# Two attention layers: the maxima over keys turned by VectorE's 32x32 transposes in place of TensorE's 128x128 transposes

## The reference

```python
q = conv1x1(xn, wq, bq).reshape(B, N, C)
k = conv1x1(xn, wk, bk).reshape(B, N, C)
v = conv1x1(xn, wv, bv).reshape(B, N, C)
scores = jnp.einsum('bnc,bmc->bnm', q, k) * scale
attn = jax.nn.softmax(scores, axis=-1)
out = jnp.einsum('bnm,bmc->bnc', attn, v).reshape(B, H, W, C)
return conv1x1(out, wp, bp) + x
```

## Time and profile before

| | |
|---|---|
| median of 3 runs | 264.88 us (264.76 to 265.24) |
| the profiled execution | 265.16 us |
| its span, first to last instruction | 263.3 us |
| granted clock of TensorE | 1.00 |
| busy: TensorE, VectorE, ScalarE, GpSimd | 257.6, 178.2, 151.3, 110.5 us |

### The profile page before, as it was taken

The page is one execution under the profiler, slowest core; times in us unless marked ns, Lnnn a source line. Parts: engine busy times, 40 slices in busy tenths (PEclk is TensorE's granted clock), DMA queues, the critical chain, the costliest instruction groups (busy, mean ns, idle before and its releaser), DMA issues.

```text
span 263.3 us, 4614 instructions
## 1 busy us (share of the span) xinstructions
PE 257.6 (98%) x1662; PEld 233.8 (89%) x1662; DVE 178.2 (68%) x437; ACT 151.3 (57%) x295; POOL 110.5 (42%) x111
## 2 busy tenths in 40 slices
PE   7799999999999999999999999999999999999995
PEld 6688889889998899889998899889998899889995
DVE  0688877886983677389876677479966667257603
ACT  3575544699984539535567529544577439542900
POOL 2010901185769019310575609510474809500940
PEclk9999999999999999999999999999999999999999
DMA  6960000000000000000000000000010000100102
GB/s 211 339 212 0 0 4 0 0 0 2 0 1 4 0 2 0 0 2 1 0 4 0 0 2 0 0 2 20 24 40 0 4 20 20 40 2 20 42 20 80
DMA packets 6989, 7.37 MB, mean 28 GB/s; under 512 B 556, under 2 KB 6712, under 8 KB 6968
## 3 DMA queue, kind: packets, MB, share of 16 engines
q1 hardware_dynamic: 6944, 7.08, 8.0%
q10 hardware_dynamic: 24, 0.01, 0.0%
HBM read 4.99 MB, written 2.10 MB: 27 GB/s over the span
## 4 chain that ended last, share of the span: by engine, by line
PE 91%; DVE 5%; DMA 2%; SPq 1%; ACT 0%; issue 0%; DVEq 0%
PE ring L942 11%; PE ring L944 11%; PE ring L943 11%; PE ring L981 11%; PE ring L983 11%; PE ring L982 11%; PE ring L928 3%; PE ring L929 3%; PE ring L930 3%; PE ring L915 3%; PE ring L917 2%; PE ring L916 2%; PE Z L831 2%; DVE S L637 2%; DMA xnat<-in_x 2%; PE X L974 1%
## 5 line engine op out<-in xcount | busy, mean ns | idle before, releaser
L291 POOL TENSOR_TENSOR P_lo<-S,P_hi 128x512 fp32r<-128x512 f32 x64 | 82.9, 1314 | 93.5 <-ACT S L406 93.3
L981 PE MATMUL ring<-V,P_hi 128*128 128x258 f32 x256 | 73.7, 288 | 0.0
L983 PE MATMUL ring<-V,P_lo 128*128 128x258 f32 x256 | 72.2, 282 | 0.0
L982 PE MATMUL ring<-V,P_hi 128*128 128x256 f32 x256 | 72.2, 282 | 0.0
L398 ACT COPY S<-ring 128x512 f32<-128x512 f32 x64 | 37.3, 590 | 44.2 <-PE ring L944 40.9
L405 ACT ACTIVATE P_hi<-S 128x512 fp32r<-128x512 f32 x64 | 40.2, 628 | 37.2 <-DVE S L637 37.2
L942 PE MATMUL ring<-t_hi,xn_lo 128*128 128x512 f32 x128 | 51.5, 402 | 0.0
L944 PE MATMUL ring<-t_hi,xn_hi 128*128 128x512 f32 x128 | 50.1, 391 | 0.0
L943 PE MATMUL ring<-t_lo,xn_hi 128*128 128x512 f32 x128 | 49.9, 390 | 0.0
L982 PEld LDWEIGHTS ring<-V,P_hi 128*128 128x128 f32 x256 | 48.4, 189 | 0.5
L981 PEld LDWEIGHTS ring<-V,P_hi 128*128 128x128 f32 x256 | 48.4, 189 | 0.5
(11 more groups left out here) (103 smaller groups left out, 342.0 us busy)
## 6 DMA issues: line engine op xcount, KB each, us to landing
xnat<-in_x SPq DMA_DIRECT2D x8, 256.0 KB, 6.2
out<-xnat SPq DMA_DIRECT2D x16, 128.0 KB, 1.7
wide<-in_vectors SPq DMA_DIRECT2D x2, 384.0 KB, 6.6
w_wq<-in_L_conv_wq SPq DMA_DIRECT2D x2, 256.0 KB, 4.4
w_wk<-in_L_conv_wk SPq DMA_DIRECT2D x2, 256.0 KB, 4.6
w_wv<-in_L_conv_wv SPq DMA_DIRECT2D x2, 256.0 KB, 6.0
w_wp<-in_L_conv_wp SPq DMA_DIRECT2D x1, 256.0 KB, 5.8
w_wp<-in_L_conv_wo SPq DMA_DIRECT2D x1, 256.0 KB, 6.3
```

Source lines behind the costliest of these rows:

```text
L291: nc.gpsimd.tensor_tensor(P_lo[:, exp_of(c, kb), :], S[:, tile_of(c, kb), :], P_hi[:, exp_of(c, kb), :].bitcast(F32), ALU.subtract).then_i ...
L981: nc.tensor.matmul(bank[:, 0:C + 2], P_hi[:, tile, mine], v[:, kb, 0:C + 2], start=(kb == 0), stop=False)
L982: nc.tensor.matmul(bank[:, 0:C], P_hi[:, tile, mine], v[:, kb, C + 2:VX], start=False, stop=False)
L983: last = nc.tensor.matmul(bank[:, 0:C + 2], P_lo[:, tile, mine], v[:, kb, 0:C + 2], start=False, stop=(kb == NB - 1))
```

## The change

The transposes of both kinds leave TensorE. `query_maxima` transposes `R` on VectorE in blocks of 32x32 into `X`, so that query `32 b + i` stands on the partitions `i`, `32+i`, `64+i` and `96+i`, with 32 of the 128 key partitions in each group of 32 partitions. A reduction leaves 16 numbers on each of 128 partitions (`quarters`), three copies bring the upper three groups of 32 partitions down to the first, and a second, small reduction gives `neg_max` on 32 partitions. `query_shift` makes `neg_less` there, adds `w` into each of the four groups of partitions, and a second block transpose, of a tile read with a step of zero, writes `X`. The bias of the queries is now wanted in that layout too, so `values_of_queries` copies `w_row` in four pieces for each chunk. The order around it changes in the first two chunks: `query_maxima(0)` stands ahead of `v_low(0, 0)`, and `group_deviation(1)`, `variance(1)` and `affine_map(1)` stand later. `X` is no longer written by TensorE in between, so its two semaphores go.

```diff
+    SQ = 32
+    BLOCKS = BANK // SQ
+    QUARTERS = P // SQ
...
+            def values_of_queries(c):
+                dve.wait_ge(dv_V, c // 2 * NB + (c % 2 + 1) * QB)
+                of_group = w_query[:, c % 2, :].rearrange("p (j g) -> p g j", g=QUARTERS)
+                for g in range(QUARTERS):
+                    last = nc.vector.tensor_copy(of_group[:, g, :],
+                                                 w_row[g * SQ:(g + 1) * SQ, (c % 2) * QB:(c % 2 + 1) * QB])
+                last.then_inc(dv_w, 1)
             def query_maxima(c):
-                dve.wait_ge(pe_R, c + 1)
-                nc.vector.tensor_reduce(neg_max[:], X[:, :].rearrange("p (j n) -> p j n", j=QB), AX_X, ALU.max,
+                dve.wait_ge(dv_R, count_R(c, NB - 1))
+                nc.vector.transpose(X[:], R[:]).then_inc(dv_turned, 1)
+                dve.wait_ge(dv_turned, c + 1)
+                nc.vector.tensor_reduce(quarters[:, 0, :], X[:, :].rearrange("p (b n) -> p b n", n=SQ), AX_X, ALU.max,
                                         negate=True).then_inc(dv_max, 1)
+                dve.wait_ge(dv_max, 3 * c + 1)
+                for g in range(1, QUARTERS):
+                    last = nc.vector.tensor_copy(quarters[0:SQ, g, :], quarters[g * SQ:(g + 1) * SQ, 0, :])
+                last.then_inc(dv_max, 1)
+                dve.wait_ge(dv_max, 3 * c + 2)
+                nc.vector.tensor_reduce(neg_max[:], quarters[0:SQ, :, :].rearrange("p g b -> p b g"), AX_X, ALU.min
+                                        ).then_inc(dv_max, 1)
             def query_shift(c):
-                dve.wait_ge(dv_V, c // 2 * NB + (c % 2 + 1) * QB)
-                w = w_row[:, (c % 2) * QB:(c % 2 + 1) * QB]
-                dve.wait_ge(dv_max, c + 1)
+                w = w_query[:, c % 2, :]
+                dve.wait_ge(dv_w, c + 1)
+                dve.wait_ge(dv_max, 3 * c + 3)
                 nc.vector.tensor_tensor(neg_less[:], neg_max[:], w, ALU.subtract).then_inc(dv_shift, 1)
-                dve.wait_ge(dv_shift, 2 * c + 1)
-                nc.vector.tensor_tensor(neg_shift[:], neg_less[:], w, ALU.add).then_inc(dv_shift, 1)
+                dve.wait_ge(dv_shift, 3 * c + 1)
+                for g in range(QUARTERS):
+                    last = nc.vector.tensor_tensor(neg_shift[g * SQ:(g + 1) * SQ, :], neg_less[:], w, ALU.add)
+                last.then_inc(dv_shift, 1)
+                dve.wait_ge(dv_shift, 3 * c + 2)
+                nc.vector.transpose(X[:], neg_shift[:, :, None].to_broadcast([P, BLOCKS, SQ])).then_inc(dv_shift, 1)
             def shifted(c, kb):
-                dve.wait_ge(pe_M, c + 1)
+                dve.wait_ge(dv_shift, 3 * c + 3)
...
-            group_deviation(1)
+            query_maxima(0)
             for m in range(QB):
                 v_low(0, m)
-                if m == 2:
-                    query_maxima(0)
+            values_of_queries(0)
             query_shift(0)
-            variance(1)
-            for m in range(QB, NB):
-                v_low(0, m)
+            v_low(0, 4)
+            v_low(0, 5)
             shifted(0, 0)
-            affine_map(1)
+            v_low(0, 6)
+            v_low(0, 7)
+            values_of_queries(1)
+            group_deviation(1)
             shifted(0, 1)
             for kb in range(1, NB):
                 running_max(1, kb)
                 if kb < NB - 1:
                     shifted(0, kb + 1)
+                if kb == 3:
+                    variance(1)
+                if kb == 4:
+                    affine_map(1)
...
                 for m in range(NB):
                     v_low(u, m)
                     if u > 1 and m in (1, 4):
                         shifted(before, 6 + m // 3)
+                for c in (first, second):
+                    values_of_queries(c)
...
             for m in range(NB):
                 values(0, m)
-                if m == 2:
-                    maxima_by_query(0)
-                    variance_of_groups(1)
-                if m == 5:
-                    shift_to_all(0)
             for kb in range(NB):
                 scores(1, kb)
+                if kb == 4:
+                    variance_of_groups(1)
             for kb in range(NB):
                 attention_by_keys(0, kb)
-                if kb == 1:
-                    maxima_by_query(1)
-                if kb == 3:
-                    shift_to_all(1)
...
                     for kb in range(NB):
                         attend(c, j, kb)
-                        if (j, kb) == (0, 4):
-                            maxima_by_query(following)
-                        if (j, kb) == (1, 1):
-                            shift_to_all(following)
```

More of the change, by code:

```diff
@@ L118, in two_attention_layers @@
         R = sb("R", [P, BANK])
-        neg_max = sb("neg_max", [P, QB])
-        neg_less = sb("neg_less", [P, QB])
-        neg_shift = sb("neg_shift", [P, QB])
+        quarters = sb("quarters", [P, QUARTERS, BLOCKS])
+        neg_max = sb("neg_max", [SQ, BLOCKS])
+        neg_less = sb("neg_less", [SQ, BLOCKS])
+        neg_shift = sb("neg_shift", [P, BLOCKS])
+        w_query = sb("w_query", [SQ, HALVES, BLOCKS])
         S = sb("S", [P, TILES, BANK])
@@ L1066, in _ @@
                         next_rows(u + 1, kb // 3)
-                attention(before, first, second_half, third_rows)
+                attention(before, second_half, third_rows)
                 for kb in range(NB):
@@ L1077, in _ @@
                         variance_of_groups(u + 1)
-                attention(first, second, next_first_half, lambda: None)
+                attention(first, next_first_half, lambda: None)
             for kb in range(NB // 2):
```

21 lines of the change are left out of this document (3 added, 18 removed).

## The result

The changed kernel takes 280.28 us (median of 4 runs, 279.62 to 280.55), the kernel before beside it 265.04 (264.76 to 265.24). The ratio is 1.0572, 95% interval 1.055 to 1.0594. The profiled execution has a span of 277.8 us against 263.3, so the traces have 14.5 of the 15.2 us to explain. Forecast were 278.0. Single executions far above the rest of their kernel (422.65 us in experiment 8, 648.89 in experiment 9, 1450.02 of the kernel before beside experiments 3, 4, 7 and 9) are left out of every time given here.

A forecast was written before the change was run, and what follows sets the result against it. TensorE, busy 98% of the span, was taken as the bound; -7.0 + 9.4 + 5.0 + 0.6 + 5.4 = +13.4 us on 265.16 gave 278 us. The forecast's own range was 274 to 283, the overall range 262.5 to 283.

The forecast's parts named there:

- Removal: TensorE's queue: 64 matmuls leave in 16 groups of four, 0.44 us each on the chain, -7.0 us.
- VectorE's chain: Per chunk, chunk 3 as example: transposes, reductions, copies and additions take 3.83 us against 1.07, 2.75 us more.
- Chunks 0 and 1: Early stage: late affine_map(1) alternates with P_lo, delays running maxima and unit 1's first values; +9.4 us with four groups gone.
- the turns: During affine_map(1): VectorE's two-source SBUF operations alternate with GpSimd's queued P_lo, about 1.4 us per VectorE operation.
- Chunks 3 and 5: Ahead of t_product(u+1, 0, 0): TensorE waits 2.5 us for xn_lo behind VectorE's longer chain, twice, +5.0 us.
- values_of_queries: Units 1 to 3: eight copies held beside GpSimd's residuals, up to 5.8 us, make maxima and statistics late; +5.4 us together.
- rival A: Copies of values_of_queries run free, only two-source operations collide with GpSimd; 272.9 us, chance 0.13.
- the Trainium skill's rule: VectorE and GpSimd lock shared SBUF ports for whole instructions; concerns VectorE's two-port modes or two SBUF inputs; carries the 5.4 us.
- Chunk 7: End of kernel: exponentials 1.5 us later delay GpSimd's last P_lo; cover 0.88, price +0.6 us.
- B (no turns): affine_map waits once for GpSimd or not at all, only VectorE's longer chain costs; +1.0, 265.9 us, chance 0.18.
- C (short chain, free ports): Nothing takes turns, chain only 1.9 us longer with fast transposes and small pieces; -2.2, 263.0 us, chance 0.15.

The follow-up runs named there:

- experiment 8: Changed kernel with 10 matmuls of ident with itself on TensorE ahead of t_product(2, 0, 0) and t_product(3, 0, 0): 278.90 us.
- experiment 9: Kernel before, with the change's VectorE operations in chunks 2, 4 and 6 only, order between chunks 0 and 1 as before: 263.67 us, ratio 0.996.
- experiment 3: Changed kernel with r0sq, r_err, rstd and gain_mean of affine_map in PSUM instead of SBUF: 278.02 us.
- experiment 4: Changed kernel with power(1) behind the first two P_lo of chunk 0 in GpSimd's queue instead of ahead of them: 278.42 us.
- experiment 7: Changed kernel with 20 matmuls of ident with itself on TensorE ahead of t_product(2, 0, 0) and t_product(3, 0, 0): 280.67 us.
- experiment 2: Kernel before, TensorE's transposes kept, with only the new order of image 1's statistics and affine map between chunks 0 and 1: 273.07 us, ratio 1.0296.
- experiment 1: Changed kernel with group_deviation(1), variance(1), affine_map(1) and variance_of_groups(1) back where they were before the change: 274.72 us, ratio 1.0362.
- experiment 5: Changed kernel with values_of_queries' copies of units 1, 2 and 3 behind the running maxima of the unit's first chunk: 281.42 us.
- experiment 6: Changed kernel with two xn_lo ahead of query_maxima(second) instead of behind query_shift(second) and output(first, 0), units 1 and 2: 278.69 us.
- experiment 12: Changed kernel, all chunks, reordered: image 1's statistics early, xn_lo ahead of maxima, statistics_of(u+1, 2) behind output(before, 3), copies moved: 271.19 us, ratio 1.0234.

## Why the prediction was right, and where its terms were not

**Removal, -7.0.** Right: the three places where nothing else changed gave 0.88, 0.88 and 0.84 for two groups, that is 0.43 each.

**VectorE's chain, 3.83 against 1.07.** 4.09 against 1.07, an increase of 3.02 where 2.75 stood (`xn_lo` starts 4.76 us behind the chain's start, before 1.75). Transposition 0.75, small pieces 0.17: of the two values weighed for each the right ones were taken, and the lower bounds (0.5 and 0.08) were not met. What is missing lies in the second transposition, 0.76 where 0.6 stood, and in the reduction of 64 columns, 0.36 to the next start where 0.25 stood.

**Chunks 0 and 1, +9.4 (+7.6 net of four groups).** 7.44 net, and experiment 2 shows that the mechanism named, GpSimd's `power(1)` ahead of P_lo and the turns, makes 7.4 us of loss without the rest of the change; experiment 1 shows that the longer chain is a cause of its own in these stages, which the forecast counts behind the turns. But the size came together from errors that cancel. The forecast had six operations in turn at 1.4, ending at 64.6 (its own terms, 0.9 and five times 1.4 from 56.35, give 64.25). Four were held, the full turns 1.22 from start to start, because the P_lo in progress runs its normal time and VectorE's operation slips in behind it; then no P_lo was left, and the six ended at 63.67. It had nothing for ScalarE's wait for a tile (3.06 us), behind which affine_map began at 58.97 and not at 56.35. And it had VectorE as the path until 82.05; instead TensorE came late by itself, since with the wait (forecast 58.8 to 65.3, found 59.14 to 64.33) its clock fell: O(0) took 2.8 us more than its waits explain (19.81 - 12.39 + 0.88 - 0.35 - 5.19).

**Chunks 3 and 5, +5.0.** The waits are 2.56 and 2.58. The step that failed is that a wait costs its own length: behind it the clock fell, 1.67 us more in each. In the ten such waits of these traces that happened eight times, so it is part of the cost, but not of every execution. The two stages cost 7.1 net where 3.2 was forecast, the largest miss of the sum.

**values_of_queries, +5.4.** The copies are held, as forecast (0.63 each, 0.16 in unit 0 and where GpSimd is idle), so rival A's premise is wrong, though its price for them, nothing, is nearer to what the runs showed, about 1.1 us, than the 5.4. The step that failed is "the first running maximum goes from 143.84 to 149.4 and with its pitch of 0.8 the last to 155.4". The copies took 5.05 us and the maxima caught up: only 1.1 us was left in unit 2 and nothing in unit 1. What TensorE then waited for was `output(3, 3)`, behind `shifted` and statistics on VectorE, and not the sum of the statistics; it waited 1.5 us. S(3) and S(5) cost 2.3: 1.1 for the copies in unit 2, and 0.6 in each unit for the chain of chunks 2 and 4, which the forecast put at nothing since it looked only at the exponentials and not at `output(1, 3)` and `output(3, 3)` behind them (experiments 5 and 9). Of the Trainium skill's rule ("SBUF — State Buffer", "SBUF: two separate sides") the half on two SBUF sources has rows in experiment 3 (0.17 us or held). The copies, one source from SBUF to SBUF, are held as its half on the two-port mode would have it; that they run in that mode no row shows.

**Chunk 7, +0.6.** TensorE waits 1.03 us for the last P_lo (267.84 to 268.87), and O(6) and O(7) cost 0.4 net in place of -0.3.

**The rivals.** B (no turns) and C (short chain, free ports) fell with the rows at 59.65 and 127.13. The stages' sum of 14.4 stands against 13.3 forecast: 3.9 too little in chunks 3 and 5, 0.7 too little in chunk 7, 2.6 too much for the copies, and 0.8 of the start and 0.2 of the early stage the other way. The mechanisms named carry the result; that the total is so near is in part luck, these errors cancelling.

What experiments 6 and 12 add is what the forecast had only for single places: the costs are not a matter of order alone. Taking the chain's 3.0 us out of TensorE's way in chunks 3 and 5 moved it to the next stages, and with all the orders together the kernel is still 2.3% slower than before. That no order of the whole change could be faster is argued from this and not shown.

## What to carry to other kernels

An engine busy for 68% of the span is not an engine with 32% to give: count the room in each stage up to the next wait of the bound engine, and move work only there. Here three chunks of eight had most of it, and the same edit that cost 5.7% gained 0.6% in them. When small operations must move, look at who else reads SBUF at the new place, and at what stands behind them in the other engines' queues. A forecast of a new wait on TensorE should carry a second price, for the clock behind it.

## What the hardware showed unexpectedly

- Held operations cost little where the engine would have waited: eight copies in 5.05 us beside the residuals cost the kernel nothing in unit 1 and 1.1 us in unit 2, eight in 1.38 us behind the maxima 1.3 in each.
- GpSimd doesn't lose by the turns with small operations: six P_lo in 7.41 us from 55.84 (1.24 each) in the changed kernel, while VectorE's operations on two columns slipped in between.
- Behind a wait of 2.6 us of TensorE the granted clock fell to 0.50 for some 3 us in 8 of 10 cases and not at all in 2, in kernels whose work just ahead of that wait is the same. What decides it is open; the 10 matmuls that filled the wait brought 1.4 us and not the 3.2 expected.
